# First block of a two-layer cross-attention kernel: key weights multiplied into the queries, five or six heads packed into the rows of a logits tile

## What is computed

```python
def _cross_attention(q_in, kv_in, wq, bq, wk, bk, wv, bv, wo, bo, bias_k, bias_v):
    qh = (q_in @ wq + bq).reshape(b, q_len, H, K)
    kh = (kv_in @ wk + bk).reshape(b, t, H, K)
    vh = (kv_in @ wv + bv).reshape(b, t, H, K)
    kh = concatenate([kh, bias_k], axis=1)
    vh = concatenate([vh, bias_v], axis=1)
    weights = softmax(einsum('bqhk,bthk->bhqt', qh, kh) / sqrt(K))
    return einsum('bhqt,bthk->bqhk', weights, vh).reshape(b, q_len, H * K) @ wo + bo
# a layer: x = x + _cross_attention(layer_norm(x), context, ...)
```

## Time and profile before

| | us |
|---|---|
| median of 3 runs | 2243.7 |
| lowest and highest run | 2242.16, 2246.68 |
| span of the profiled execution | 2244.8 |
| TensorE busy in it (12468 matmuls) | 2160.7 |
| VectorE busy | 1558.1 |
| ScalarE busy | 1247.0 |
| GpSimd busy | 822.3 |

### The profile page before, as it was taken

One profiled execution on the slowest core, in us unless ns is written; L12 is line 12 of the kernel. 1 busy time (PEld: TensorE's weight loads), 2 busy tenths in 40 slices (PEclk: granted clock), 3 DMA queues, 4 the chain that ended last, 5 costly groups with the idle time before them and its releaser, 6 DMA issues.

```text
span 2244.8 us, 36949 instructions
## 1 busy us (share of the span) xinstructions
PE 2160.7 (96%) x12468; PEld 2097.8 (93%) x12468; DVE 1558.1 (69%) x3631; ACT 1247.0 (56%) x2956; POOL 822.3 (37%) x754
## 2 busy tenths in 40 slices
PE   7999999999999999999999999999999989898999
PEld 6999999999999999999999999998999878786999
DVE  7777788777778877776887777787445577678241
ACT  5555555555555555554655555556366476567464
POOL 4314444241344424234442423442556311022355
PEclk9999999999999999999999999999999999899999
DMA  4657445565745555464555546454453756755243
GB/s 139 168 138 179 99 116 102 123 150 138 179 101 113 103 124 125 83 151 95 119 102 126 123 85 150 101 113 74 126 166 112 188 144 175 206 149 134 70 124 112
DMA packets 161447, 287.77 MB, mean 128 GB/s; under 512 B 35312, under 2 KB 92784, under 8 KB 161264
## 3 DMA queue, kind: packets, MB, share of 16 engines
q1 hardware_dynamic: 161264, 285.41, 53.1%
HBM read 240.32 MB, written 28.64 MB: 120 GB/s over the span
## 4 chain that ended last, share of the span: by engine, by line
PE 82%; DVE 4%; ACT 4%; DMA 4%; issue 2%; POOL 2%; SPq 1%; ACTq 0%; POOLq 0%; DVEq 0%
PE bank L873 77%; PE bank L966 3%; DMA k<-k_parts 2%; DMA ctxN_raw<-in_ctx 2%; POOL mring L808 1%; ACT prob L1389 1%; PE bank L1146 1%; DVE prob L1722 1%; DMA stage<-in_fb 1%; PE bank L1135 1%; DVE ln_c L1607 1%; SPq L676 0%; DVE qs L1554 0%; DVE ctxT L1558 0%; POOL mring L806 0%
## 5 line engine op out<-in xcount | busy, mean ns | idle before, releaser
L873 PE MATMUL bank<-ctxT,kring 128*128 128x362 f32 x3456 | 632.0, 330 | 6.6 <-DVE kT L1554 5.5
L873 PEld LDWEIGHTS bank<-ctxT,kring 128*128 128x128 f32 x3456 | 589.2, 190 | 9.6 <-POOL mring L808 6.1
L808 POOL TENSOR_TENSOR mring<-stage,mring 128x512 fp32r<-128x512 f32 x325 | 443.9, 1372 | 165.3 <-ACT mring L1275 148.1
L873 PE MATMUL bank<-pT,ctxN 128*128 128x400 f32 (+1 forms) x2304 | 471.2, 352 | 0.3 <-DVE U L1558 0.3
L806 POOL TENSOR_SCALAR mring<-stage 128x512 fp32r<-128x512 f32 x205 | 143.5, 700 | 856.8 <-PE bank L873 712.8
L873 PEld LDWEIGHTS bank<-pT,ctxN 128*128 128x128 f32 (+1 forms) x2304 | 408.7, 189 | 1.8 <-issue 0.6
L873 PE MATMUL bank<-hT,mring 128*128 128x400 f32 x1608 | 320.1, 348 | 7.7 <-POOL mring L808 4.5
L873 PE MATMUL bank<-U,mring 128*128 128x400 f32 x1536 | 303.3, 348 | 8.1 <-issue 6.4
L873 PEld LDWEIGHTS bank<-hT,mring 128*128 128x128 f32 x1608 | 294.9, 189 | 14.1 <-POOL mring L808 7.3
L873 PEld LDWEIGHTS bank<-U,mring 128*128 128x128 f32 x1536 | 275.3, 188 | 10.3 <-issue 7.9
L1275 ACT ACTIVATE kT<-bank,cols 128x361 fp32r<-128x361 f32 (+1 forms) x288 | 160.7, 558 | 211.3 <-PE bank L873 211.2
(11 more groups left out here) (103 smaller groups left out, 2954.1 us busy)
## 6 DMA issues: line engine op xcount, KB each, us to landing
ctxN_raw<-in_ctx SPq DMA_DIRECT2D x256, 192.0 KB, 3.7
ctxT_raw<-in_ctx SPq DMA_DIRECT2D x64, 724.0 KB, 7.8
k<-k_parts SPq DMA_DIRECT2D x96, 181.0 KB, 3.7
stage<-in_wk SPq DMA_DIRECT2D x64, 256.0 KB, 4.9
stage<-in_wq SPq DMA_DIRECT2D x64, 256.0 KB, 4.6
stage<-in_wv SPq DMA_DIRECT2D x64, 256.0 KB, 4.1
stage<-in_wo SPq DMA_DIRECT2D x64, 256.0 KB, 2.7
stage<-in_fa SPq DMA_DIRECT2D x64, 256.0 KB, 2.6
```

What stands on the lines that cost most here:

```text
L808: nc.gpsimd.tensor_tensor(lo, src, f32(hi), ALU.subtract).then_inc(S.w_ready, 1)
L873: mm = pe.matmul(dst, parts_l[a], parts_r[b], start=first and k == 0, stop=last and k == len(order) - 1)
```

## The change

The logits are (Q Wk^T) times the context instead of Q times (context Wk)^T. For each head the key weights (now stored transposed) are multiplied into the 400 query columns: fold, 4 chunks x 3 matmuls of 400 columns, written to QU. The logits of a tile are then 4 x 3 matmuls over the 361 columns of the raw context ctxT. As the context no longer depends on the head, the rows of a logits tile can come from several heads: the rows of 5 heads (500 per batch) make 4 tiles of 125, those of 6 heads 5 tiles of 120. A stage has three groups of 5, 5 and 6 heads, 12 groups in all. Key bias: it adds the same number to all context logits of a row and falls out of the softmax, except against the extra key, which now is bias_k less bk. The extra key's logits are made by extra_logits: for each tile two matmuls of 4 columns, whose weights are 125 or 120 columns of the queries; VectorE masks and adds them (extra_select, three instructions per group) and puts one column into the bank ahead of the logits of each tile (put_extra).

All projections (queries and folded keys of this group, values and output of the last one) stand in one stretch between the groups, in the order of projections(). They use banks 0 to 2 in turn; the output projection adds all heads of a group up in banks 4 to 7, head by head. ScalarE makes the high parts of k and o weights, GpSimd of q and v; GpSimd makes the low parts of all, and also of ctxN in three batches of four. There is one ring of four weight tiles. In a group, step i has the logits of tile i, the transposes of tile i-2 (two banks now) and value sums by sum_step: with 5 heads one unit per step, 9 matmuls of 500 columns; with 6 heads two passes of 9 matmuls of 300 columns, two units in most steps. p0_row has one buffer. ctxT is split in groups 0 and 3 only and saved; all other groups load the two saved parts (1.48 MB per batch). qT and the value parts share their place with pT. The second block keeps its work, with kT, key weights and mask at other addresses and without the unused column 0.

The core of the diff (each engine's sequence follows the same order; spread_p0, put_extra and the steps are shown for one engine):

```diff
-GN = 16
-NU = GN * 16
-LAG = 3
+GROUP_HEADS = [5, 5, 6]
+TILE_ROWS = {5: 125, 6: 120}
+NG = 12
+MAXH = 6
+BROWS = MAXH * LQ
+LAG = 2
...
+def projections(G):
+
+    now, before = heads(G), heads(G - 1)
     items = []
...
+    if now:
+        items.append(("q", G, 0))
+    if before:
+        items.append(("v", G - 1, 0))
+    for s in range(max(now, before)):
+        if s + 1 < now:
+            items.append(("q", G, s + 1))
+        if s < now:
+            items.append(("k", G, s))
+        if s == now - 1:
+            items.append(("e", G, 0))
+        if s + 1 < before:
+            items.append(("v", G - 1, s + 1))
+        if s < before:
+            items.append(("o", G - 1, s))
     return items
...
+def sum_step(G, b, c, k):
+
+    n = tiles_of(G)
+    return n * (b + 1) + LAG + (c if n == 4 else [0, 0, 1, 1, 2, 2, 3, 4][2 * c + k])
...
 def by_scalar(key):
 
-    return key[0] == "b" and key[1] % NF > 0 or key[0] == "a" and key[1] % NF > 2
+    return key[0] in "ko" or key[0] == "b" and key[1] % NF > 0 or key[0] == "a" and key[1] % NF > 2
...
-        p0_row = sb("p0_row", [1, 2, ROWS], F32)
+        p0_row = sb("p0_row", [1, BROWS], F32)
...
-        M_BANK, T_BANK = 5, 4
+        M_BANK, N_BANK, E_BANK = 5, 0, 3
+        T_BANK = [4, 5]
         U_BANK = [6, 7]
-        V_BANK = [5, 6, 7, 5]
-        O_LAST = [5, 6, 7, 4]
+        O_BANK = [4, 5, 6, 7]
...
+        def proj_bank(key):
+            return bank[PROJ_AT[key] % 3][:, 0:ROWS]
...
-            def spread_p0(r):
+            def spread_p0(G, b):
 
-                G, b = divmod(r, NB)
-                sp.wait_ge(S.p0_copied, HG * r + HG)
+                sp.wait_ge(S.p0_copied, last_tile(G, b))
...
+            def proj_bank_free(key):
+
+                n = PROJ_AT[key]
+                if n >= 3:
+                    pe.wait_ge(S.proj_done, n - 2)
...
+            def fold(G, h):
+
                 key = ("k", G, h)
+                tile_ready(key)
+                pe.wait_ge(S.proj_done, PROJ_AT["q", G, h, 0] + 1)
+                for c in range(DC):
+                    proj_bank_free(("k", G, h, c))
+                    split_mms(proj_bank(("k", G, h, c)), w_cols(key, c), [q_head(p_, h) for p_ in range(2)],
+                              True, True).then_inc(S.proj_mm, 1)
+
+            def extra_logits(G):
...
+                for b in range(NB):
+                    for j in range(n):
...
+                        for p_ in range(2):
+                            mm = pe.matmul(bank[E_BANK][0:tile_rows(G), at:at + 4], qT[:, p_, first:last],
+                                           extra_k[:, layer, h:h + 2, :].rearrange("p h k -> p (h k)"),
+                                           start=p_ == 0, stop=p_ == 1)
...
+            def logits(n):
...
+                pe.wait_ge(S.e_put, n + 1)
+                first, last = tile_columns(G, b, j)
+                for c in range(DC):
+                    mm = split_mms(bank[2 + n % 2][0:tile_rows(G), 2:LT + 2], [QU[:, p_, c, first:last] for p_ in range(2)],
+                                   ctxT_c(i, c), c == 0, c == DC - 1)
+                mm.then_inc(S.s_mm, 1)
...
             def turned_high(n):
-                r, h = divmod(n, HG)
+                G, b, j = TILES[n]
                 act.wait_ge(S.t_mm, n + 1)
-                high(p_rows(pT[:, r % 2, 0, :], h), turned(bank[T_BANK])).then_inc(S.pt_hi, 1)
-                if h == 0 and r >= 2:
-                    act.wait_ge(S.p0_in[(r - 2) % NB], 16 * ((r - 2) // NB + 1))
-                high(p0_row[0:1, r % 2, h * LQ:(h + 1) * LQ], bank[T_BANK][0:1, 0:LQ]).then_inc(S.p0_copied, 1)
+                high(turned_to(G, b, j, 0), turned_from(n)).then_inc(S.pt_hi, 1)
+                if j == 0 and NB * G + b:
+                    before = NB * G + b - 1
+                    act.wait_ge(S.p0_in[before % NB], 16 * (before // NB + 1))
+                size = tile_rows(G)
+                high(p0_row[0:1, j * size:(j + 1) * size], bank[T_BANK[n % 2]][0:1, 0:size]).then_inc(S.p0_copied, 1)
...
+                for i in range(group_steps(G)):
+                    if i < n:
+                        maximum(first + i)
+                    if i + 2 < n:
+                        put_extra(first + i + 2)
+                    if LAG <= i < n + LAG:
+                        turned_low(first + i - LAG)
+                    if i < n:
+                        normalise(first + i)
...
+                    for b, c, k in sums_at(G, i):
+                        value_sum_low(G, b, c, k)
```

More of the change, by code:

```diff
@@ new lines @@
+PROJ = [projections(G) for G in range(NG + 1)]
+PROJ_OUT = []
+for items_ in PROJ:
+    for kind_, G_, h_ in items_:
+        if kind_ in "qv":
+            PROJ_OUT.append((kind_, G_, h_, 0))
+        elif kind_ == "k":
+            PROJ_OUT += [(kind_, G_, h_, c_) for c_ in range(DC)]
+PROJ_AT = {key: n for n, key in enumerate(PROJ_OUT)}
+PROJ_HIGH = list(itertools.accumulate(key[0] != "v" for key in PROJ_OUT))
+HEAD_AT = {("v", G, h): sum(heads(g) for g in range(G)) + h for G in range(NG) for h in range(heads(G))}
```

1045 lines of the change are left out of this document (536 added, 509 removed).

## The result

The changed kernel takes **2637.0 us** (median of four runs, 2635.8 to 2638.1) against 2244.3 for the kernel before beside it: ratio 1.1743, 95% interval 1.1726 to 1.1761. The forecast was 2427, with a range to 2510.

A forecast was written before the change was run, and what follows sets the result against it. The first block was taken to be bound by TensorE's matmuls and what each costs. 2244.8 - 61 + 42 + 16 + 4 + 5 + 152 + 25 = 2428 us, stated as 2427; range 2325 to 2510.

The forecast's parts named there:

- TensorE's queue, -61: First block: priced matmuls, with fewer logits but added folded keys and extra logits, sum to 1504 us against 1565: -61 us.
- Narrow matmuls save nothing: Rival: 300 columns cost what 400 cost, 174 ns, and the extra logits 189: 2500 us; chance 0.05.
- New waits, +42: Projection stretches: folded-key chunks wait for copies out of three shared banks, 0.70 us for 52 keys, 0.5 for 12: +42 us.
- Transition, +16: After each stretch, VectorE's last work and put_extra delay the first logits tile by 1.3 us, 12 times: +16 us.
- The +4 beside it: Ends of the four 6-head groups: 300-column units wait for copies of two banks, 0.18 us six times each: +4 us.
- The wait that decides, +152: Batch ends: ScalarE waits for the single p0_row's transfer, TensorE stalls; 56 us in 5-head, 96 in 6-head groups: +152 us.
- L: Time for the probability row's transfer to land: 11.1 us with 5 heads, 13.0 us with 6.
- context splits in two stretches: Part of the +5 us for start and end of the block: context splits in two stretches cost +4 us.
- Nothing, but see the transfers below: Key contexts arrive split, 1.48 MB instead of 0.74 per batch, four or five tiles ahead: costed at nothing.
- Slow clock, +25: TensorE's low clock behind stalls at batch ends: 12 x 1.6 us plus half of 8 x 1.6: +25 us.
- weights bind: Rival: in the stretches ScalarE waits on weights, 0.25 us for 256 tiles: +64, 2491 us; chance 0.15.
- faster: Rival: the row's spread is covered and the stretches' copies keep up, leaving the saved columns: 2208 us; chance 0.05.

The follow-up runs named there:

- one_row_memory: Changed kernel, one p0_row kept; the row goes to memory and a step later in one transfer to all 128 partitions: 2319.5 us, 1.0320 of the kernel before.
- version by head: memory128_four with the extra logits in runs of 8 small matmuls ahead of each folded key but the first: 2244.1 us, 0.9989 of the kernel before.
- four banks: Changed kernel with four banks in turn for the projections instead of three, extra logits taking a place in the turn: 2588.6 us, 1.1520 of the kernel before.
- row_in_place: Changed kernel with the row copied to each batch's own place in partition 0 of p0_all and sent from there to 127 partitions: 2512.0 us.
- memory128_four: Changed kernel with the row in its place in p0_all, sent through memory to 128 partitions, context loads issued first, four projection banks: 2272.4 us.

## Why the prediction was wrong, step by step

The direction was right, and so was the wait for the row: the forecast had a loss of 183 us and named it, and it came out near its size. What failed is the step on transfers, which gave the loads behind the row's transfer no term, and the price of the slow clock. one_row_memory, which takes the row through memory, gives 318 of 393 us back. The size was short by 207 us. In the sums of the first table: 326 idle where the steps had 219 (42 + 16 + 4 + 5 + 152), and 65 busy where they had -36 (-61 + 25). By step:

- **"TensorE's queue, -61"**: short by 23. The version by head, which has the same matmuls and hardly any low clock, is busy 1524 us against 1562: -38. Of the 23, 18 are a fault of bookkeeping: 1504 was a sum of prices, and I set it against 1565 measured; by the same prices before is 16 x 96.7 = 1547, and the step -43. The rule of the Trainium skill on the gap between matmuls ("TensorE: Matmul & The Clock Gate", Back-to-back issue gap), which by the prediction would have made this step about 20 us better, did not come out: the measured step is worse than the priced one. The prices held: 0.214 us for 500 columns (0.217), 0.136 for 300 (0.135 to 0.141), and 48.5 us for the small matmuls by head (47.2). In the changed kernel the small matmuls took 57, part of them at the low clock. "Narrow matmuls save nothing" is dead.
- **"New waits, +42"**: 56.5 us. The distance to the displaced bank was the cause, as four banks show; the wait comes in two parts (0.60, then 0.27 or 0.80).
- **"Transition, +16"**: 19.3 us of waits ahead of first logits, 1.1 to 1.4 in the 5-head groups (2.25 in the first group) and 1.9 to 2.3 in those of 6 heads, where nothing stands between the extra logits and the first tile. The +4 beside it, for the ends of the 6-head groups, was 10.7.
- **"The wait that decides, +152"**: L was right (11.1 and 13), and so were the 6-head stalls (8.5, 6.6 and 7.4 against 8.8, 7.6 and 7.6), 90 us in all against 96. The 5-head ones, with the short waits behind them, were 55.5 against 56, but that is partly luck: the third boundary has no logits as cover (2.91 us instead of 1.0), the second had under 0.8, and in groups 0 and 3 another wait took the place of the first two. Together 146 us. That other wait is for the raw contexts' splits, which queued behind the blocked ScalarE (33.7 us, 4 times; the forecast had 4 us, for "context splits in two stretches").
- **"Nothing, but see the transfers below"**, said of the key contexts, while the chunks for the value sums have no term at all: this is the step that failed. I followed the row's transfer to the one engine that waits for it, and not to what stands behind it in SyncE's queue. The fourth chunk of the last batch came some 7 us late at the end of all twelve groups (78 us of idle time), and the change had put the row ahead of the chunk, which alone costs the kernel before 109 us. Of the queues that the transfer stands in I had counted only ScalarE's.
- **"Slow clock, +25"**: 103 us (busy 1627 against 1524). The earlier trace rows gave 1.6 us for one stall, and I applied it to twenty, eight of them at half. By the trace's clock records the low clock took some 2.3 us behind each of the twelve 6-head stalls and 1.7 behind each of the fourteen of 3 us, 52 in all; and it stood in three places that I had not priced, 38 us in and behind the extra logits, 23 behind the late chunks and 10 behind the raw contexts (these shares add up, with 11 for the rest, to 135, somewhat more than the 103 that show in busy). Of the part at the extra logits the version by head gives back 24 (busy 1548 to 1524).

Together: 23 + 78 (clock) + 107 (idle) = 208. The 107 are 78 for the late chunks, 30 for the raw contexts, 14 at the folds, 7 at the ends of the 6-head groups and 3 at the first logits, less 6 for the row and some 18 for waits of the kernel before that went away. (The low end that the forecast gives itself, 2320, lies outside its range as stated, 2325; nothing hangs on it.) The rivals: "weights bind" did not come (2.8 us of waits for weights), and "faster" was nearly what the same arithmetic gives with the row through memory, four banks and extra logits by head: no gain, 83 us idle against 44 take back the 38.

What stays open: which form of the transfer takes the time. From one partition to 128, from one to 127 and from memory to 127 all took 11 to 13 us; only from memory to 128 took 3.4. Only 127 and 128 partitions were tried, and the source in one partition was not tried with the bytes of fewer targets, nor the row's transfer from another engine's queue than the loads'. That a row on one DMA engine holds loads that use the others too is seen (a chunk behind it in row_in_place was there 12.6 us after the row's issue), not explained by a run. The remaining 83 us of idle time were not worked on.

## What to carry to other kernels

Price a transfer three times: for who waits on its landing, for whose buffer it holds, and for what is issued behind it in the same queue. When a buffer is halved, check the wait against the shortest steps it can meet (here 4.4 and 2.4 us, not the mean of 6.1). Compare sums of prices with sums of prices, and give every stall that is new its time at the low clock as well.

## What the runs showed that I had not expected

- The same 250 to 300 KB land in 11.1 us from one partition and in 3.4 from memory; a hop of 2 KB through memory is worth it (-318 us in the changed kernel).
- A transfer from one partition to 127 had the DMA engines 0.06 busy at 25 GB/s, one to 128 had them 0.90 busy at 28, and the chunk behind was there 12.6 and 11.5 us after the row's issue. From memory, with four banks in both, 127 partitions make 2389 us and 128 make 2272.
- In the changed kernel the granted clock was 0.50 behind all twelve runs of 32 or 40 matmuls of 4 columns, without a long gap in TensorE's work; in memory128_four behind six of twelve, and behind two it stayed at 1.00. Behind all 52 runs of 8 in memory128_four_byhead it was 1.00.
- One wait hides another: taking the row's away raised ScalarE's waits for chunks from 88 to 250 us.
